# Mixture of experts in two parts: each token's row in DRAM goes from 130 to 144 values

## The chip, the cores and the metric

The kernel runs on one core of one Trainium2 chip. The metric is device time in microseconds (us) of one execution. The engines are named as in the profile: PE (matrix multiplication; PEld is its loading of weights), DVE (vector), ACT (activations), POOL (GpSimd), SP (which here only issues DMA transfers).

## The reference, cut to what matters

The program is four layers, each as `x = x + layernorm(layer(layernorm(x)))`, over 16 x 256 = 4096 tokens of 128 fp32 values: differential attention, two rounds of window attention with a feed-forward block, a state-space scan, and a mixture of experts. Only the last one is touched:

```python
xt = x.reshape(-1, D)                        # 4096 tokens, D = 128
logits = xt @ router_w.T                     # 8 experts
topk_vals, topk_idx = jax.lax.top_k(logits, TOP_K)          # TOP_K = 2
g = jax.nn.sigmoid(topk_vals)
g = g / (g.sum(axis=-1, keepdims=True) + 1e-10)
for e in range(E):                                          # E = 8, H = 256
    ge = jnp.sum(jnp.where(topk_idx == e, g, jnp.zeros_like(g)), axis=-1)
    h = jax.nn.silu(xt @ w_gate[e]) * (xt @ w_up[e])
    out = out + ge[:, None] * (h @ w_down[e])
```

## The kernel before

A token goes to two of eight experts, so the kernel sorts tokens by expert through DRAM. It holds 32 tiles of 128 tokens, in eight groups of four tiles; groups 0 to 4 are part 0, groups 5 to 7 part 1.

**The row.** What is sorted is a row of `ROW = D + 2 = 130` fp32 values, 520 bytes: the 128 normalised values of the token (written by ACT into the tile `pay`, L647 called from `outer_apply`), the token's number (column 128, written for all tokens by one DVE copy, L1881) and the number of its first expert (column 129, written by DVE in `choose`, L1753). The DRAM tensor `mx_rows` has 9 x 4096 = 36864 such rows: a region for each expert in each part, and one spare for slots that hold no expert's tile.

**The fill.** Before the sorting, all rows of `mx_rows` are set to a blank row: SP issues nine transfers (L2301) of 4096 rows each from the tile `mx_blank` during the first layer, right behind the loads of the weights. POOL waits for all nine (`filled`) before it sends the first token row.

**Sending.** In the mixture DVE, PE and ACT work out group by group where each token's two rows go (`choose`, `place`, `ranks`). POOL then issues eight indirect transfers a group (L1662), each of which writes 128 rows from `pay` to the rows that `mx_posu` names: 64 such transfers in all. Between groups POOL raises variances to the power -1/2 for two layernorms (L620), which ACT needs for the next groups' rows.

**The experts.** A table that DVE makes lists 80 slots: for each, an expert and the 128 rows that it works on. SP loads slot i (L1613: 128 rows into one of 16 buffers of the ring `mx_xin`) once the part's rows have been sent (`sent`), and from the 17th on once the buffer's former tile has been turned by PE (`x_full`) and its numbers read by DVE (`aimed`, L1848 to L1853). PE turns two tiles at a time (L2095), ACT moves them out of PSUM (L1965), then come gate and up (PE L2102, ACT L1973, DVE L1860), the turning of h (PE L2110, ACT L1979), down (PE L2120), and DVE's move of the result into `mx_y` (L1867). POOL writes the result by an indirect transfer of 128 rows of 512 bytes into `mx_results` (L1692). Sends of the last group and a half stand between POOL's first slots.

**The end.** When all results of a part have landed, SP fetches them (L1619, L1620), ACT and DVE weigh, sum and normalise them, and SP stores the output (L1624).

All orders are written out by hand, one program for each engine; each waits on semaphores only. There is no scheduler.

Of the kernel before, what the change touches and what calls it, by code (L numbers as in the profile page):

```python
# [12 lines left out]
D = 128  # L13
# [78 lines left out]
def apart(eng, scratch):  # L92

    eng.tensor_tensor(scratch, scratch, scratch, ALU.mult)
# [1366 lines left out]

ROW = D + 2
PAD = 1e6
FIRST = (0, 5, GROUPS)
PART_TILES = [NT * (FIRST[p + 1] - FIRST[p]) for p in range(2)]
# [22 lines left out]
def dispatch_constants(sb):  # L1491
    c = {}
    for k, shape in (("tri", [P, P]), ("ones", [P, P]), ("region", [P, 2, NE]), ("upto", [P, NE, NE]),
                     ("tile_no", [P, SLOTS]), ("tile_rows", [P, TILES]), ("trash", [P, SLOTS]), ("blank", [P, ROW]),
                     ("token", [P, TILES])):
        c[k] = sb("mx_" + k, shape)
    for k, n in (("count", SLOTS), ("place", SLOTS), ("number", TILES)):
        c[k] = sb("mx_" + k, [P, n], I32)
    return c

def mixture_of_experts(nc, X, F, out, rows, results, consts, c, w, ws, states, filled, fills):
# [10 lines left out]
    with ExitStack() as ctx:  # L1513
# [6 lines left out]

        pay = sb("pay", [P, TILES, ROW])
        top = sb("top", [P, TILES, 8])
# [5 lines left out]
        idf = sb("idf", [P, TILES, 2])  # L1528
# [21 lines left out]
        targetu = sb("targetu", [P, SLOTS], U32)  # L1550
        xin = sb("xin", [P, RING, ROW])
        xT = sb("xT", [P, 2, 2, P])
# [14 lines left out]
        applied, added, paid, first_named = (sem(n) for n in ("applied", "added", "paid", "first_named"))  # L1567
# [17 lines left out]
        def of(g):  # L1585
            return slice(g * NT, (g + 1) * NT)

        def part_of(g):
            return 0 if g < FIRST[1] else 1

        def seen_at(g):

            return g + part_of(g)
# [17 lines left out]
        def _(sp):  # L1611
# [16 lines left out]
            for part in range(2):  # L1628
                sp.wait_ge(listed, part + 1)
                for i in range(START[part], START[part + 1]):  # L1630
                    if i % SHARE == 0:
                        _, values = nc.values_load_multi_w_load_instructions(
                            c["place"][0:1, i:i + SHARE], engines=(mybir.EngineType.SP,), min_val=0,
                            max_val=(NE + 1) * TILES * P - P, skip_runtime_bounds_check_because=BOUND)
                        for k, v in enumerate(values):
                            at[i + k] = v
                    if i == START[part]:
                        sp.wait_ge(sent[part], 16 * 2 * PART_TILES[part])
                    if i >= RING:
                        sp.wait_ge(x_full, (i - RING) // 2 + 1)  # L1640
                        sp.wait_ge(aimed, (i - RING) // SHARE + 1)
                    load(i)
                    if i == START[1] + RING + 2:
                        fetch(0)
# [66 lines left out]
        def _(dve):  # L1711
            own_steps = Steps(dve, own)

            def outputs(g):

                for b in (2 * g, 2 * g + 1):
                    dve.wait_ge(o_full, b + 1)
                    dve.tensor_tensor(F[:, QT + b * QT:QT + (b + 1) * QT, :],
                                      psO[:, b % 2, 0:T].rearrange("p (t n) -> p t n", t=QT),
                                      dv[:, :].unsqueeze(1).broadcast_to([P, QT, D]), ALU.add).then_inc(o_used, 1)  # L1720
                dve.wait_ge(o_used, 2 * g + 2)
                inner.statistics(dve, g)
# [8 lines left out]
            def choose(g):  # L1731

                dve.wait_ge(r_full, g + 1)
                ins = dve.tensor_copy(lo[:, of(g), :], psR[:, 0:NT * NE].rearrange("p (t e) -> p t e", t=NT))
                ins.then_inc(r_used, 1)
                dve.wait_ge(r_used, g + 1)
                apart(dve, APART["dve"])
                for t in range(g * NT, (g + 1) * NT):
                    ins = dve.max(top[:, t, :], lo[:, t, :])
                own_steps.mark(ins)  # L1740
                own_steps.last()
                apart(dve, APART["dve"])
                for t in range(g * NT, (g + 1) * NT):
                    ins = dve.max_index(idx[:, t, :], top[:, t, :], lo[:, t, :])
                own_steps.mark(ins)
                own_steps.last()
                own_steps.mark(dve.tensor_copy(idf[:, of(g), :], idx[:, of(g), 0:2]))
                own_steps.last()
                own_steps.mark(dve.tensor_tensor(
                    hot[:, g, :, :, :], eid[:, :].unsqueeze(1).unsqueeze(1).broadcast_to([P, 2, NT, NE]),  # L1750
                    idf[:, of(g), :].rearrange("p t c -> p c t").unsqueeze(3).broadcast_to([P, 2, NT, NE]),
                    ALU.is_equal))
                dve.tensor_copy(pay[:, of(g), D + 1:ROW], idf[:, of(g), 0:1]).then_inc(first_named, 1)  # L1753
                own_steps.last()
                dve.tensor_tensor(both[:, g, :, :], hot[:, g, 0, :, :], hot[:, g, 1, :, :], ALU.add)\
                   .then_inc(hot_ready, 1)
                dve.wait_ge(hot_ready, g + 1)
                own_steps.mark(dve.tensor_reduce(inc[:, g, :], both[:, g, :, :].rearrange("p t e -> p e t"),
                                                 axis=AX.X, op=ALU.add))
                own_steps.last()  # L1760
                dve.tensor_tensor(seen[:, seen_at(g) + 1, :], seen[:, seen_at(g), :], inc[:, g, :], ALU.add)\
                   .then_inc(seen_ready, 1)
# [115 lines left out]

            dve.memset(seen[:, 0, :], 0.0)
            dve.memset(seen[:, seen_at(FIRST[1]), :], 0.0).then_inc(seen_ready, 1)  # L1880
            dve.tensor_copy(pay[:, :, D:D + 1], c["token"][:, :].unsqueeze(2)).then_inc(numbered, 1)  # L1881
            outputs(0)
            outputs(1)
# [8 lines left out]
            outer.shifts(dve, 1)  # L1892
            residual(2)
            choose(0)
            place(0)
            for g in range(FIRST[1]):
                outer.shifts(dve, g + 2)
                inner.shifts(dve, g + 3)
                choose(g + 1)
                if g + 4 < GROUPS:  # L1900
                    outputs(g + 4)
                place(g + 1)
                if g + 2 == FIRST[1]:
                    need_tiles(0)
                    tiles_of_experts(0)
                    rows_of_tiles(0)
                residual(g + 3)
            gates(0)
            choose(LATE - 1)
            place(LATE - 1)  # L1910
            outer.shifts(dve, LATE)

            gate_up(0)
            for i in range(SLOTS + 1):
# [18 lines left out]
                if i - 5 in SUM_AT:  # L1933
                    g = SUM_AT[i - 5]
# [97 lines left out]
        def _(pe):  # L2032
# [46 lines left out]
            def load_experts(n):  # L2079
                _, values = nc.values_load_multi_w_load_instructions(  # L2080
                    c["count"][0:1, n * SHARE:(n + 1) * SHARE], engines=(mybir.EngineType.PE,), min_val=0,
                    max_val=NE - 1, skip_runtime_bounds_check_because=BOUND)
                for k, v in enumerate(values):
                    chosen[n * SHARE + k] = v
# [79 lines left out]
def build(nc, ins, consts_in, out, stop=None):  # L2164
    with ExitStack() as ctx:
# [64 lines left out]
        mx = dispatch_constants(sb)  # L2230
        rows = nc.dram_tensor("mx_rows", ((NE + 1) * TILES * P, ROW), FP32).ap()
        results = nc.dram_tensor("mx_results", (2 * TILES * P + SLOTS * P, D), FP32).ap()
# [3 lines left out]
        with nc.Block() as block:  # L2236
# [7 lines left out]
            def _(pool):  # L2244
# [8 lines left out]
                pool.memset(mx["blank"][:, D:D + 1], PAD)  # L2253
                pool.memset(mx["blank"][:, D + 1:ROW], -1.0).then_inc(blanked, 1)
                pool.memset(mx["ones"][:, :], 1.0)
# [174 lines left out]
```

## Time and profile before

| | |
|---|---|
| Time before, median of 3 runs | 2056.2 us (2054.87 to 2056.44) |
| The profiled execution's own time | 2068.7 us |
| Its span, first to last instruction | 2066.9 us |
| PE, DVE, ACT, POOL busy | 84%, 75%, 66%, 43% of the span |
| The mixture of experts in the span | from about 1765 us to the end |
| TensorE clock granted, mean | 0.925 |

The profile is of one execution, which took 12.5 us longer than the median of the timed runs. The shares of busy time are means over four layers with different limits; for this change what counts is the fill, which lies in the first layer, and the last 300 us.

### The profile page before, as it was taken

How to read it: one execution, taken by the hardware profiler on the slowest of the kernel's cores; microseconds unless marked ns; L12 is line 12 of the kernel's file. 1: busy time of each engine (PE TensorE's matmuls, PEld its weight loads, DVE VectorE, ACT ScalarE, POOL GpSimd, SP SyncE). 2: the span in 40 equal slices, each digit the busy share in tenths (PEclk: the TensorE clock that was granted, in tenths of full speed). 3: DMA queues.
4: the chain of work that ended last, by engine and by line, in shares of the span. 5: the costliest groups of instructions: out<-in, count | busy, mean ns of one | idle time of the engine just before them, and what ended most of it. 6: DMA issues, size and time to landing. Idle time of an engine off the chain costs nothing. (4 is left out here: it accounts for less than half of the span.)

```text
span 2066.9 us, 39567 instructions
## 1 busy us (share of the span) xinstructions
PE 1733.7 (84%) x12418; PEld 1135.9 (55%) x12484; DVE 1555.1 (75%) x4202; ACT 1371.4 (66%) x4730; POOL 880.0 (43%) x819
## 2 busy tenths in 40 slices
PE   4999999999999945999998786999997765647883
PEld 2555555555555523777776443777776432544552
DVE  2988889988889866999996565999996564753353
ACT  2888888888888853888886224888886235323454
POOL 3555655556555543333332123333332122475553
PEclk9999999999999977999999897999999897659996
DMA  7990000000000000000000100000000100012242
GB/s 206 189 183 2 2 2 2 2 2 2 1 2 2 2 0 6 16 12 16 16 11 20 30 14 6 16 11 17 17 13 19 30 13 1 16 54 78 76 115 77
DMA packets 103935, 66.98 MB, mean 32 GB/s; under 512 B 27954, under 2 KB 95154, under 8 KB 103730
## 3 DMA queue, kind: packets, MB, share of 16 engines
q1 hardware_dynamic: 99122, 54.94, 13.2%
q0 software_dynamic: 4608, 9.51, 1.4%
q8 instruction: 104, 1.70, 0.4%
q14 instruction: 101, 0.83, 0.1%
HBM read 20.03 MB, written 30.77 MB: 25 GB/s over the span
## 5 line engine op out<-in xcount | busy, mean ns | idle before, releaser
L411 ACT ACTIVATE a_E<-a_psS,a_nm 128x128 f32<-128x128 f32 (+1 forms) x1028 | 419.8, 429 | 31.0 <-DVE a_nm L245 28.4
L216 POOL TENSOR_SCALAR a_aT<-a_dT 128x384 f32<-128x384 f32 x256 | 310.1, 1211 | 298.8 <-PE a_psO L529 187.3
L245 DVE TENSOR_REDUCE a_nm<-a_psS 128x2 f32<-128x256 f32 (+1 forms) x514 | 260.2, 547 | 44.7 <-PE a_psS L496 44.1
L492 PE MATMUL a_psS<-a_kT,a_qm 32*128 32x128 f32 (+1 forms) x2064 | 240.6, 351 | 5.7 <-issue 3.7
L270 DVE SCALAR_TENSOR_TENSOR a_d<-a_E,a_cf 128x128 f32<-128x128 f32 (+1 forms) x512 | 218.7, 468 | 28.1 <-DVE a_cf L259 1.9
L411 ACT ACTIVATION_READ_ACCUMULATOR a_E<-a_psS,a_nm 128x1 f32 x1028 | 220.3, 214 | 0.0
L830 POOL TENSOR_TENSOR b1rn<-b1ss,minus_half 128x16 f32<-128x16 f32 x36 | 107.2, 2977 | 223.5 <-DVE b1ss L866 223.5
L830 POOL TENSOR_TENSOR b0rn<-b0ss,minus_half 128x16 f32<-128x16 f32 x36 | 107.2, 2977 | 221.9 <-DVE b0ss L866 221.9
L420 ACT ACTIVATE a_dT<-a_psT 128x384 f32<-128x384 f32 x256 | 127.0, 496 | 74.6 <-PE a_psT L505 72.0
L492 PEld LDWEIGHTS a_psS<-a_kT,a_qm 32*128 32x128 f32 x2064 | 136.6, 186 | 56.1 <-issue 36.0
L505 PE MATMUL a_psT<-ident,a_d 128*128 128x128 f32 x768 | 132.2, 281 | 6.6 <-DVE a_d L270 0.5
L1692 POOL DMA_INDIRECT mx_results<-mx_y,mx_targetu x80 | 77.2, 965 | 74.1 <-DVE mx_y L1867 57.2
L505 PEld LDWEIGHTS a_psT<-ident,a_d 128*128 128x128 f32 x768 | 87.7, 141 | 35.0 <-DVE a_d L270 29.0
L496 PE MATMUL a_psS<-causal,identb 128*128 128x256 bf16 x516 | 101.9, 279 | 0.0
L964 ACT ACTIVATE b0E<-b0psS,b0nm 128x128 f32<-128x128 f32 x260 | 92.0, 377 | 10.0 <-DVE b0nm L894 10.0
L964 ACT ACTIVATE b1E<-b1psS,b1nm 128x128 f32<-128x128 f32 x260 | 92.0, 377 | 8.7 <-DVE b1nm L894 8.7
L1077 PE MATMUL b0psQ<-wqk,b0hT 128*128 128x512 f32 x148 | 80.5, 670 | 17.0 <-DVE b0part L875 12.0
L1077 PE MATMUL b1psQ<-wqk,b1hT 128*128 128x512 f32 x148 | 80.6, 670 | 16.8 <-DVE b1part L875 11.3
L2102 PE MATMUL mx_psG<-m_experts,mx_xT 128*128 x160 | 85.8, 619 | 8.8 <-ACT mx_xT L1965 8.5
L1860 DVE TENSOR_TENSOR mx_h<-mx_psG,mx_sl 128x256 f32<-128x256 f32 x80 | 33.9, 424 | 75.6 <-ACT mx_sl L1973 43.3
L1046 PEld LDWEIGHTS b1psS<-b1kT,b1qm 128*128 128x128 f32 x528 | 71.8, 197 | 18.2 <-issue 16.3
L518 PE MATMUL a_psO<-a_dT,a_vp 128*32 128x256 f32 x516 | 81.2, 393 | 0.6 <-ACT a_dT L420 0.6
(359 smaller groups left out, 4425.4 us busy)
## 6 DMA issues: line engine op xcount, KB each, us to landing
mx_rows<-mx_blank SPq DMA_DIRECT2D x9, 2080.0 KB, 30.8
mx_xin<-mx_rows SPq DMA_DIRECT2D x80, 65.0 KB
b0v<-b0v SPq DMA_DIRECT2D x34, 128.0 KB, 2.3
b1v<-b1v SPq DMA_DIRECT2D x34, 128.0 KB
F<-mx_results SPq DMA_DIRECT2D x8, 256.0 KB, 4.6
mx_second<-mx_results SPq DMA_DIRECT2D x8, 256.0 KB, 5.0
out_dram<-X SPq DMA_DIRECT2D x8, 256.0 KB, 2.4
mx_results<-mx_y,mx_targetu POOLq DMA_INDIRECT x80
```

The costliest lines, as they stand in the source:

```text
L216: pool.tensor_scalar(aT[:, s, :], dT[:, s, :], 0.0, None, ALU.max).then_inc(positived.sem, 1)
L245: ins = dve.tensor_reduce(nm[:, s, t, :], psS[:, s, :, (0, P)[t]:(P, 384)[t]], axis=AX.X, op=ALU.max, negate=True)
L270: ins = dve.scalar_tensor_tensor(out=d[:, s, c0:c1], in0=E[:, s, 1, c0:c1], scalar=cf[:, s, t:t + 1], in1=E[:, s, 0, c0:c1], op0=ALU.mult, ...
L411: ins = act.activation(E[:, s, m, c0:c1], psS[:, s, m, c0:c1], ACT.Exp, bias=nm[:, s, t, m:m + 1], accum_out=Z[:, p, h, t, m:m + 1])
L420: act.activation(dT[:, s, :], psT[:, s, 0:384], ACT.Copy).then_inc(evaced.sem, 1)
L492: pe.matmul(psS[:, s, m, c0:c1], qm[rows, p, a, r, t * P:(t + 1) * P], kT[rows, p, a, 0:c1 - c0], start=(t == 0), stop=False)
L496: ins = pe.matmul(diagonal, identb[:, :], causal[:, :].unsqueeze(1).broadcast_to([P, 2, P]), start=False, stop=True)
L505: ins = pe.transpose(psT[:, s, c * P:(c + 1) * P], d[:, s, c * P:(c + 1) * P], ident[:, :])
L830: pool.tensor_tensor(rn[:, t, :], ss[:, t, :], minus_half[:, 0:2 * H], ALU.pow).then_inc(rn_ready.sem, 1)
L964: ins = act.activation(E[:, s, n, :], psS[:, s, n * P:(n + 1) * P], ACT.Exp, bias=nm[:, s, n:n + 1], accum_out=Z[:, s, n:n + 1])
L1077: ins = pe.matmul(psQ[:, n * W:(n + 1) * W], hT[:, p, t * P:(t + 1) * P], wqk[:, n * W:(n + 1) * W], start=True, stop=True)
L2102: pe.matmul(psG[:, i % 2, :], xT[:, i // 2 % 2, i % 2, :], of_expert(i, 0, DOWN), start=True, stop=True)\
```

## The change

`ROW` becomes `D + 16 = 144` values, 576 bytes, in `mx_rows`, `pay`, `mx_blank` and `mx_xin`. Columns 130 to 143 carry nothing. Column 129 is now addressed as one column instead of as the rest of the row, and a new DVE memset at the start of the mixture sets the 14 new columns of all 32 tiles of `pay` to zero. The memset of `mx_blank`'s last columns (POOL, at the start of the program) becomes 15 columns wide instead of one.

```diff
-ROW = D + 2
+ROW = D + 16
...
-                dve.tensor_copy(pay[:, of(g), D + 1:ROW], idf[:, of(g), 0:1]).then_inc(first_named, 1)
+                dve.tensor_copy(pay[:, of(g), D + 1:D + 2], idf[:, of(g), 0:1]).then_inc(first_named, 1)
...
             dve.memset(seen[:, 0, :], 0.0)
             dve.memset(seen[:, seen_at(FIRST[1]), :], 0.0).then_inc(seen_ready, 1)
+            dve.memset(pay[:, :, D + 2:ROW], 0.0)
             dve.tensor_copy(pay[:, :, D:D + 1], c["token"][:, :].unsqueeze(2)).then_inc(numbered, 1)
```

The order of instructions is the same on every engine but for this one on DVE. The piece of the difference below is DVE's at the start of the mixture; 128x32x14 is partitions, tiles and new columns.

```order
 L1879 MEMSET mx_seen 128x8
 L1880 MEMSET mx_seen 128x8
-L1881 COPY mx_pay<-mx_token 128x32
+L1881 MEMSET mx_pay 128x32x14
+L1882 COPY mx_pay<-mx_token 128x32
 L1718 TENSOR_TENSOR F<-mx_psY,s_wD 128x256 x2
```

The memset has come between the two small ones and the copy of the tokens' numbers; everything behind it moves down one line. The transfers are as many as before, in the same places: 9 of the fill, 64 sends, 80 loads, all with 144 values a row in place of 130.

## Rows read from the trace of the kernel before

**Rows 1.** The page: span, busy time and share of the engines, DMA queues.

```profile
span 2066.9 us, 39567 instructions
PE 1733.7 (84%) x12418; PEld 1135.9 (55%) x12484; DVE 1555.1 (75%) x4202; ACT 1371.4 (66%) x4730; POOL 880.0 (43%) x819
...
q1 hardware_dynamic: 99122, 54.94, 13.2%
q0 software_dynamic: 4608, 9.51, 1.4%
```

**Rows 2.** The chain that ended last: start, length, what.

```profile
1789.56 1.24 POOL mx_rows L1662
...
1835.78 0.97 POOL mx_rows L1662
...
2036.15 0.96 POOL mx_results L1692
```

**Rows 3.** Timeline from part 0's last send to PE's first expert tile.

```profile
1849.40 0.96 POOL L1662 DMA_INDIRECT mx_rows<-mx_pay,mx_posu  x1 [0.30 <-issue]
...
1851.85 20.07 SPq L1613 DMA_DIRECT2D mx_xin<-mx_rows  x16
...
1858.41 1.11 PE L2048 MATMUL mx_psX<-ident,mx_pay 128*128 128x128 f32 x4 [2.75 <-issue]
...
1863.94 2.07 PE L2102 MATMUL mx_psG<-m_experts,mx_xT 128*128 x2 [3.98 <-ACT mx_xT L1965]
```

**Rows 4.** Timeline of PE where the loop over slots has no pauses.

```profile
1973.20 0.38 PE L2095 MATMUL mx_psT<-ident,mx_xin 128*128 128x128 f32 x2
...
1979.75 0.38 PE L2095 MATMUL mx_psT<-ident,mx_xin 128*128 128x128 f32 x2
```

**Rows 5.** ACT's waits, 1866 to 2034 us: total us, times, longest.

```profile
ACT mx_xT L1965 <- PE mx_psT L2095: 11.2, 20, 1.6
...
ACT mx_xT L1965 <- remote: 5.2, 3, 2.3
```

**Rows 6.** SP's waits, 1780 us to the end: total us, times, longest.

```profile
SPq L1641 <- DVE mx_targetu L1853: 21.5, 4, 8.7
```

**Rows 7.** Timeline of SP, the fill's issues.

```profile
46.60 95.05 SPq L2301 DMA_DIRECT2D mx_rows<-mx_blank  x9
```

**Rows 8.** DMA queue, 90 to 150 us: packets, MB, share of 16 engines.

```profile
q1 hardware_dynamic: 21482, 11.13, 123.0%
```

**Rows 9.** L411, ACT's exponentials: stretch, us, busy (count), PEclk, DMA share, GB/s.

```profile
83.40:126.90 43.50, 27.59 (x128) 1.00 1.26 186
213.90:257.40 43.50, 27.63 (x129) 1.00 0.01 2
```

**Rows 10.** Timeline of DVE at the mixture's start.

```profile
1765.70 0.07 DVE L1879 MEMSET mx_seen<- 128x8 f32 x1 [0.64 <-PEq L1362]
1765.72 0.20 DVE L1881 COPY mx_pay<-mx_token 128x32 f32<-128x32 f32 x1
...
1766.38 0.87 DVE L1718 TENSOR_TENSOR F<-mx_psY,s_wD 128x256 f32<-128x256 f32 x2 [0.46 <-PE mx_psY L2039]
```

**Rows 11.** Groups by form: busy us, mean ns, idle before.

```profile
L918 DVE MEMSET b0qm<- 128x4096 f32 x1 | 3.5, 3472 | 0.8 <-issue 0.8
...
L336 DVE MEMSET a_psO<- 128x256 f32 x1 | 0.3, 272 | 0.4 <-PEq L2236 0.4
...
L1692 POOL DMA_INDIRECT mx_results<-mx_y,mx_targetu x80 | 77.2, 965 | 74.1 <-DVE mx_y L1867 57.2 <-issue 16.9
```

**Rows 12.** The sends' line: ns least/median/most, first and last start.

```profile
L1662 POOL DMA_INDIRECT mx_rows<-mx_pay,mx_posu x64: 957/962/1299, 1789.6 to 1946.0; - x64
```

**Rows 13.** DMA queue, 1852 to 1878 us, loads of `mx_xin`: columns as above.

```profile
q1 hardware_dynamic: 3024, 1.40, 25.5%
```

**Rows 14.** DMA queue, 2058 to 2062 us, stores of 512-byte rows.

```profile
q1 hardware_dynamic: 773, 0.38, 33.6%
```

**Rows 15.** DMA queue, 1851.8 to 1855 us.

```profile
q1 hardware_dynamic: 554, 0.26, 45.5%
```

## The prediction

> **What bounds the kernel now.** I start with the page. PE is busy for 84% of the span and the rows' transfers for little: the queue that carries the fill and the loads took 13.2% of the time of 16 DMA engines, the queue of POOL's indirect transfers 1.4% [rows 1]. These are means over four layers, and only two stretches hold the changed rows: the fill in the first layer, and the mixture from 1765 us on. So the chain of work that ended last comes next. In the mixture it first runs through POOL: from 1789.56 us to the end of the piece at 1835.78 it is POOL issuing sends and, between groups, raising variances to a power. It then passes to DVE, PE and ACT, and in the experts mostly through PE, until POOL's last result at 2036.15 us [rows 2].
>
> The reader should look at two places. The first is the hand-over from sending to experts. Part 0's last send is issued by 1850.36 us (1849.40 + 0.96), SP issues the first load at 1851.85, PE still turns the last group of tokens at 1858.41, and its first expert matmul starts at 1863.94 [rows 3]. The second is the loop over slots. Where it has no pauses PE turns a pair of tiles, and four tiles later another: 1979.75 - 1973.20 = 6.55 us, 1.64 us a tile [rows 4]. For 80 tiles that is 131 us, but the loop goes from 1863.94 to 2037.11 us, 173 us. The 42 us between are pauses and added work. A part that could have to do with loaded rows is ACT's wait for the turned tiles, 11.2 us in 20 waits and another 5.2 us whose releaser the trace does not tell [rows 5]. SP itself is ahead of PE there: its waits before a load are 21.5 us on DVE's numbers of a share eight tiles back [rows 6], so a load is issued many tiles before its use.
>
> **The fill.** Nine transfers with 36864 rows in all are issued by SP from 46.60 us for 95 us [rows 7]. From 90 to 150 us there is little else: 123.0% of 16 engines x 60 us over 21482 packets is 55.0 ns a packet, one row each, and 36864 of them take 103 us [rows 8]. The trace has no row of 576 bytes. Lower bound: the stores of 512-byte rows took 33.6% x 16 x 4 us / 773 = 27.8 ns a packet [rows 14]; scaled to 576 bytes 31.3 ns, a fill of 59 us. Upper bound: 55.0 x 576/520 = 60.9 ns, 114 us. I take no value between, because neither costs anything: POOL waits for the fill only before its first send at 1789.56 us, and the attention beside the fill keeps its pace. In a stretch of 43.5 us ACT did 128 exponentials in 27.59 us with the DMA share at 1.26, and 129 in 27.63 us with it at 0.01 [rows 9]. If that cover were gone the fill would cost its own change, -44 to +11 us; nothing in the rows makes it go.
>
> **The memset.** It writes 32 x 14 = 448 values a partition on DVE. Two memsets give the slope: 272 ns for 256 values, 3472 ns for 4096, 0.833 ns a value, so 448 values take 0.43 us [rows 11]. Upper bound: short runs may cost more; the copy behind it, with 32 runs of one value, takes 0.20 us, and adding that whole gives 0.63 us. DVE now idles 0.46 us, waiting for PE, between that copy and its first real work at 1766.38 [rows 10]. So 0 to 0.17 us shows; I take 0.05 us and count it in full. Behind it stands DVE's first sum and with it all of the mixture, so a memset that outlasts the cover delays everything by what is over. POOL's memset of 15 columns in place of one lies at the program's start, beside the loads of the inputs: nothing.
>
> **The sends.** Of 64, 32 lie on the chain (four groups of eight between 1789.56 and 1836 us) [rows 2]. Each holds POOL for 962 ns at 520 bytes a row [rows 12]; the indirect transfers of 512-byte rows take 965 ns in the mean [rows 11]. POOL's time goes by rows and not by bytes as far as these two sizes tell, and both have 128 rows. I take nothing. Upper bound: a time in proportion to bytes would be 962 x 56/520 = 0.10 us a send, 3.3 us for 32 and 4.1 us for part 0's 40. A gain is excluded on POOL: shorter rows were no cheaper.
>
> **The loads and landings.** A load gives each of 16 engines eight rows. From 1852 to 1878 us a packet took 25.5% x 16 x 26 us / 3024 = 35.1 ns [rows 13], a load 0.28 us of an engine. With the bounds of above it becomes 8 x 31.3 = 0.25 us or 8 x 38.9 (35.1 x 576/520) = 0.31 us: -0.03 to +0.03 us. I take 0 for the loads, since they are ahead of PE. The first ones are the closest: by 1855 us 554 packets, some four loads of 128 rows, had moved [rows 15], and PE is not free before 1858.41 [rows 3], so 3 us cover a change of hundredths. The last send's landing is as short a piece, eight rows an engine at 6 ns more, 0.05 us, behind the same cover; I add it as the only other term.
>
> The Trainium skill speaks against the pad here ("DMA: Bandwidth & Descriptors", section "How a descriptor splits into AXI transactions"): a read is charged in beats of 32 bytes from the 256-byte boundary below its start. By my estimate from that page, rows of 520 bytes, whose starts move by 8 bytes, cost 20.5 beats in the mean, and rows of 576 bytes, whose starts move by 64, cost 21.0; alignment to 64 bytes would then buy nothing on reads, and a load would go from 0.28 to 0.29 us. The stores above, aligned to 512 bytes, are cheaper per packet than either kind of 520-byte row, which fits an alignment cost but does not say that 64 bytes are enough. By page or by row the sum is the same to 0.1 us.
>
> **Sum.** 0.05 + 0.05 = 0.1 us. The profiled execution took 2068.7 us and would take 2068.8. It is 12.5 us above the median of the runs, of which I know no cause in these terms, so I carry the difference over unscaled: 2056.2 + 0.1 = 2056.3 us. A measurement of this kernel tells about 0.2%, 4 us, from no change.
>
> **Rivals.**
>
> *Everything hidden (the forecast), 0.80.* It includes the case that the padding does not do what it is for, that packets take as long a byte as before, since neither end of the packets' price reaches the end of the program. Its own range is -1 to +1.5 us: 2055 to 2058.
>
> *Slower: POOL's sends grow with the row, 0.08.* The place is L1662 on the chain. It decides from 4.1 us / 32 = 0.13 us a send. Against it stand the two equal durations; for it, that 512 and 520 bytes are so near that they exclude no step above them. In proportion to bytes it gives 2059.6 to 2060.4 us, just short of telling; if a row of 576 bytes were written as two pieces and a send cost twice 0.96 us, 32 x 0.96 = 31 us and 2087 us.
>
> *Faster: late rows are behind part of the loop's pauses, 0.12.* The waits for turned tiles are 16.4 us [rows 5], the loop's loss 42 us. Rows of 55 and 35 ns beside 28 ns say that something about 520-byte rows is dear, and if their transfers also held up completions that PE waits for, a quarter to a half of 16.4 us would go: 2048 to 2052 us. Against it: SP is 8 tiles or more ahead [rows 6], that is 8 x 1.64 = 13 us for a transfer of 0.3 us, and the loop runs without pauses at 1973 us.
>
> **How the numbers follow.** The likeliest case gives 2056.3 us. From the range I leave out the double send and the farther half of the faster case, together about 1 in 8: 2050.5 to 2061 us. Faster by over 0.2% is 0.10: of the third case 0.02 stay within, at its 2052 us. Slower is 0.06: of the second case 0.02 stay within, at 2059.6 us. Within is the rest, 0.84.
>
> **What would show it.** In the profile of the changed kernel: a DVE memset of about 0.43 us at the mixture's start, with the first sum (L1718) at most 0.2 us later behind it; sends still at 0.96 us; a fill of 36864 rows at 31 to 61 ns each, with the attention's stretches unchanged; first load about 1.5 us behind the last send; the pause-free loop still at 1.64 us a tile. The prediction is wrong if sends are longer than 1.06 us, if the waits of ACT for turned tiles fall or rise by more than 4 us, or if the attention beside the fill moves by more than 1 us in 43.5.

## The result: 0.36% faster, through a layer that the diff does not name

| | before | after |
|---|---|---|
| Median | 2055.7 us (6 runs, 2054.87 to 2056.57) | 2047.84 us (6 runs, 2046.78 to 2050.49) |
| Ratio, 95% interval | | 0.9964 [0.9951, 0.9977] |
| Profiled execution | 2068.7 us | 2049.57 us |

The forecast was no change. The time fell by 7.9 us, past the low end of the range by 2.7 us.

First the page of the changed kernel, beside [rows 1].

```profile
span 2047.8 us, 39568 instructions
PE 1736.7 (85%) x12418; PEld 1142.2 (56%) x12484; DVE 1553.2 (76%) x4203; ACT 1371.8 (67%) x4730; POOL 879.9 (43%) x819
...
q1 hardware_dynamic: 99122, 57.58, 10.9%
q0 software_dynamic: 4608, 9.97, 1.5%
```

More bytes took less of the DMA engines' time: 10.9% in place of 13.2%. The padding does make the fill cheaper. The next three views are SP's timeline at the fill, the queue from 60 to 100 us, and ACT's exponentials beside and behind the fill, the first and third as in [rows 7] and [rows 9].

```profile
47.26 68.21 SPq L2302 DMA_DIRECT2D mx_rows<-mx_blank  x9
```
```profile
q1 hardware_dynamic: 20554, 11.79, 113.8%
```
```profile
83.40:126.90 43.50, 27.63 (x129) 1.00 1.04 273
213.90:257.40 43.50, 27.60 (x128) 1.00 0.01 2
```

The issues of the fill take 27 us less, and a packet takes 113.8% x 16 x 40 / 20554 = 35.4 ns. But the attention beside the fill has the pace that it has without one, so none of this reaches the end.

DVE at the mixture's start, the sends' line, and the hand-over to the loads, beside [rows 10, 12, 3]:

```profile
1763.78 0.07 DVE L1879 MEMSET mx_seen<- 128x8 f32 x1 [0.64 <-PEq L1362]
...
1763.93 0.43 DVE L1881 MEMSET mx_pay<- 128x448 f32 x1
1764.28 0.13 DVE L1882 COPY mx_pay<-mx_token 128x32 f32<-128x32 f32 x1
1764.46 0.87 DVE L1718 TENSOR_TENSOR F<-mx_psY,s_wD 128x256 f32<-128x256 f32 x2
```
```profile
L1662 POOL DMA_INDIRECT mx_rows<-mx_pay,mx_posu x64: 957/962/1301, 1787.6 to 1927.5; - x64
```
```profile
1847.47 0.96 POOL L1662 DMA_INDIRECT mx_rows<-mx_pay,mx_posu  x1 [0.30 <-issue]
```
```profile
1849.96 1.96 SPq L1613 DMA_DIRECT2D mx_xin<-mx_rows  x4
```

From the first memset to the first sum it is 0.68 us, as before. A send is 962 ns, as before. From part 0's last send to the first load it is 2.49 us against 2.45. The stages that the prediction looked at are as it said. So where did 7.9 us come from?

**A trap in the pair of profiles.** The two spans differ by 19.1 us, and the loop over slots seems to give most of it. These are the rows of that loop, from the first to the last gate matmul: before, after, and then two kernels from the experiments, one that gains (z alone moved) and one that doesn't (mixture alone moved).

```profile
1863.94:2031.88 167.94, 141.66 (x722) 89.56 (x723) 76.99 (x298) 81.93 (x237) 92.12 (x96) 0.98 0.31 87
```
```profile
1857.40:2012.62 155.22, 143.22 (x721) 94.43 (x722) 75.10 (x298) 82.28 (x237) 95.85 (x99) 0.93 0.35 99
```
```profile
1856.37:2030.50 174.13, 148.21 (x721) 94.81 (x722) 76.40 (x298) 82.64 (x237) 94.21 (x98) 0.93 0.30 85
```
```profile
1864.34:2019.81 155.47, 143.52 (x722) 94.48 (x723) 74.95 (x298) 82.45 (x237) 95.63 (x99) 0.93 0.33 95
```

Over all profiles the loop, from the start of the first gate matmul to the start of the last, is 155 us or 168 to 178 us long. Among the sixteen profiles of the experiments, which of the two it is went with the set of kernels that shared a chip, not with the kernel. In the two sets in which the kernel before had medians of 2076.2 and 2074.3 us, all eight profiles show the long loop; in the two with 2052.9 and 2054.0 us, all eight show the short one. The 12.7 us between the first pair look like such a difference and no part of the 7.9 us: the kernel before, whose profile has the long loop, took 2055.7 us as the median of its runs, like the sets with the short one. What makes the loop long in a set is not known. What the timed runs tell from one another had to be found with kernels timed side by side.

### The profile page after: what moved, and what is told of

It is laid out like the page before. It is cut to its first block and busy times, and to the rows that moved or that the text cites. A ratio compares the mean times of both kernels' runs of the same rounds, so it can differ in the third digit from the quotient of the medians.

```text
span 2047.8 us, 39568 instructions
## 1 busy us (share of the span) xinstructions
PE 1736.7 (85%) x12418; PEld 1142.2 (56%) x12484; DVE 1553.2 (76%) x4203; ACT 1371.8 (67%) x4730; POOL 879.9 (43%) x819
## 3 DMA queue, kind: packets, MB, share of 16 engines
q1 hardware_dynamic: 99122, 57.58, 10.9%
## 5 line engine op out<-in xcount | busy, mean ns | idle before, releaser
L411 ACT ACTIVATE a_E<-a_psS,a_nm 128x128 f32<-128x128 f32 (+1 forms) x1028 | 419.9, 429 | 30.4 <-DVE a_nm L245 27.8
L411 ACT ACTIVATION_READ_ACCUMULATOR a_E<-a_psS,a_nm 128x1 f32 x1028 | 220.5, 215 | 0.0
L1046 PEld LDWEIGHTS b0psS<-b0kT,b0qm 128*128 128x128 f32 x528 | 71.9, 197 | 18.2 <-issue 16.3
```

Of the source, the lines that this page charges most:

```text
L411: ins = act.activation(E[:, s, m, c0:c1], psS[:, s, m, c0:c1], ACT.Exp, bias=nm[:, s, t, m:m + 1], accum_out=Z[:, p, h, t, m:m + 1])
```

## The experiments

Ratios are to runs of the kernel before on the same chip.

### Padded rows in DRAM, or padded tiles in SBUF?

The kernel before once more, for the resolution of what follows.

> The kernel before, unchanged, as the measure of what a repeat does. All theories: ratio 1.000 within 0.001. Its profile also tells whether the pauses of the loop over slots (41 us above 1.64 us a tile in the first profile, with SP instructions of 0.7 us) belong to the kernel or to that one profiled execution: if to the kernel, the loop again takes about 168 us from first to last gate matmul; if to the execution, some 10 us less.

Measured: 0.9996 [0.9986, 1.0006]. Its loop over slots took 170.2 us, so by the expectation the pauses would belong to the kernel. The sets with the short loop show that one repeat was not enough to say so: there a kernel whose mixture has other places in SBUF and nothing else changed took 155.5 us.

Wide tiles, narrow rows in DRAM:

```diff
+WIDE = D + 16
-... ("blank", [P, ROW]),
+... ("blank", [P, WIDE]),
-        pay = sb("pay", [P, TILES, ROW])
+        pay = sb("pay", [P, TILES, WIDE])
-        xin = sb("xin", [P, RING, ROW])
+        xin = sb("xin", [P, RING, WIDE])
```

with the memsets of the change, and every transfer moving columns 0 to 129 alone.

> The rows in DRAM keep 130 values and every transfer moves 130; only the tiles in SBUF are 144 wide, with the new memset, so all tiles lie where the change puts them. Theory A (the gain comes from rows that start and end on 64 bytes in DRAM): ratio 1.000, fill at 55 ns a row. Theory B (the gain comes from where the tiles lie in SBUF, 32 bytes and more further on): ratio 0.996, fill at 55 ns a row.

Measured: 0.9967 [0.9954, 0.9980]. The whole gain is there with 520-byte rows in DRAM.

Rows of 568 bytes (`ROW = D + 14`):

> The change with 14 new values a row (142, 568 bytes: 8 bytes short of a multiple of 64) in place of 16. Theory A (64-byte multiples in DRAM): ratio 1.000 or a little above, a fill of 55 ns a row or more, 60 ns at most. Theory B (place in SBUF): 0.996. A third theory, that wider rows help by themselves: 0.996 with the fill's price anything.

Measured: 0.9970 [0.9957, 0.9982].

Rows of 544 bytes (`ROW = D + 8`):

> The change with 8 new columns... 136 values a row, 544 bytes, a multiple of 32 bytes but not of 64. Theory A in its 64-byte form: like 130 values, ratio 1.000, fill about 55 ns a row. If 32 bytes are enough: ratio 0.996 and a fill of about 31 ns a row, as with 144. Theory B (place in SBUF): 0.996 whatever the fill.

Measured: 1.0004 [0.9993, 1.0015]. No account by the alignment of DRAM rows sorts these: 520 in DRAM gains, 568 gains, 544 does not, although its fill is cheap too (37.6 ns a row). Theory B as written missed the last one as well: it took for granted that 136 values also move the tiles. With 576 every tile of the layers, all allocated behind it, stands 32 bytes further: what started 32 bytes past a multiple of 64 now starts at one, and the other way round.

### Is it the place of the later tiles?

An unused tile of 32 bytes does the move by itself. In the kernel before:

```diff
         mx = dispatch_constants(sb)
+        sb("gap32", [P, 8])
```

> The kernel before (rows of 130 values, no memset) with one unused tile of 32 bytes a partition right behind the dispatch constants, so that every tile after it lies 32 bytes further in SBUF, as in the changed kernel. Theory P (the place of the later tiles in SBUF is what counts): ratio 0.9965 to 0.997, below 0.998. Theory D (the padded rows and their transfers count): 1.000 within 0.001. Theory L (what counts is the larger tile itself, or its memset): 1.000.

Measured: 0.9954 [0.9941, 0.9967]. The same line in the changed kernel, which takes the move back:

> The changed kernel (rows of 144 values, memset) with the same 32-byte tile, so that every later tile is back at the place modulo 64 bytes that it had before the change. Theory P: the gain is gone, ratio 1.000 within 0.001. Theory D and theory L: the gain stays, 0.9965.

Measured: 0.9998 [0.9989, 1.0006]. Its fill is the cheap one (36864 rows in about the same 68 us) and its memset is there. This is the change as the prediction saw it, and it is worth nothing. Theory P holds; theories D and L fall. (Theories have new letters in each group of experiments; each expectation says what its letters mean.)

### Which layer, which tile?

The gap at the start of the mixture's stack only:

> The kernel before with a 32-byte tile at the start of the mixture's stack alone: only the mixture's tiles move by 32 bytes. If the mixture's tiles carry the gain of theory P: 0.997. If the layers ahead do: 1.000; if the mixture loses by the move and the others gain, over 1.000. Theory D: 1.000.

Measured: 0.9999 [0.9989, 1.0009]. The gap around the other layers:

```diff
-        differential_attention(nc, X, consts, wA, load_later)
+        with nc.sbuf_tensor("gap32a", [P, 8], FP32):
+            differential_attention(nc, X, consts, wA, load_later)
...
+            with nc.sbuf_tensor("gap32b", [P, 8], FP32):
                 normalise_all(nc, "n0", X, F, minus_half)
                 for l in range(2):
                     window_attention(nc, f"b{l}", F, consts, wB[l])
...
                     feed_forward(nc, f"f{l}", F, consts, wF[l])
```

> The kernel before with a 32-byte tile around the attention and around the window and feed-forward layers alone: their tiles move by 32 bytes, those of the state-space layer and of the mixture stay. If these layers carry the gain of theory P: 0.997, with the feed-forward layers near 95.9 us instead of 98.2 and a window layer near 362.1 us instead of 363.6 in the profile. If the mixture does: 1.000. Theory D: 1.000.

Measured: 0.9966 [0.9953, 0.9979]. The gain lies ahead of the mixture. In the profiles the feed-forward layers differ, and the first difference in them is their start. There SP brings the first tokens from the tile `F` into the tile `z` in three transfers: half of the channels straight, the other half one token further, and the token that this leaves over. DVE can't begin before they land. SP's, DVE's and PE's timelines at the start of the first feed-forward layer in the kernel before:

```profile
1131.47 0.71 SPq L1222 DMA_DIRECT2D f0z<-F  x1
1132.23 0.87 SPq L1223 DMA_DIRECT2D f0z<-F  x1
1133.15 7.00 SPq L1224 DMA_DIRECT2D f0z<-F  x1
```
```profile
1143.03 0.87 DVE L1257 BATCH_NORM_STATS2 f0st<-f0z 128x6 f32<-128x128 f32 x4 [12.61 <-DMA f0z<-F]
```
```profile
1146.89 1.11 PE L1322 MATMUL f0psX<-ident,f0xn 128*128 128x128 f32 x4 [16.93 <-DVE f0xn L1272]
```

And in the changed kernel:

```profile
1135.19 0.71 SPq L1222 DMA_DIRECT2D f0z<-F  x1
1135.95 0.87 SPq L1223 DMA_DIRECT2D f0z<-F  x1
1136.87 6.50 SPq L1224 DMA_DIRECT2D f0z<-F  x1
```
```profile
1145.46 0.87 DVE L1257 BATCH_NORM_STATS2 f0st<-f0z 128x6 f32<-128x128 f32 x4 [11.32 <-DMA f0z<-F]
```
```profile
1149.32 1.11 PE L1322 MATMUL f0psX<-ident,f0xn 128*128 128x128 f32 x4 [15.65 <-DVE f0xn L1272]
```

From the first issue to DVE's statistics: 11.56 us before, 10.27 after. The rest of the way to PE is the same 3.86 us. `z` is the first tile of its layer; by the sizes of the tiles ahead of it, it starts 32 bytes past a multiple of 64 in the kernel before and at a multiple in the changed one. So `z` alone was moved, with the tiles behind it put back:

```diff
+        sb("gapa", [P, 8])
         z = sb("z", [P, 2, NT, D])
+        sb("gapb", [P, 8])
         st = sb("st", [P, NT, 6])
```

> The kernel before with 32 bytes ahead of the tile z of each feed-forward layer and 32 bytes behind it: z, the target of that layer's transfers from F, starts at a multiple of 64 bytes, and every other tile keeps its place modulo 64. Theory Z (rows of 256 bytes that DMA writes to a place 32 bytes off a multiple of 64 cost more, and each feed-forward layer starts with them): z's first landing 1.3 us earlier, with the slower clock behind it some 2.2 us less per layer, ratio 0.9978 to 0.998, all that the feed-forward layers have to give. Theory A (engines read or write their tiles at another pace at the other place): 1.000, since no other tile moves.

Measured: 0.9968 [0.9958, 0.9978]. Everything moved except `z`:

> The kernel before with every tile after the dispatch constants moved by 32 bytes except the tile z of the feed-forward layers, which stays at 32 modulo 64. Theory Z: 4.4 us short of the kernel with all tiles moved, ratio 0.9975 to 0.998, with the feed-forward layers at 98.2 us as before. Theory A: 0.9955, as with all tiles moved.

Measured: 0.9989 [0.9978, 1.0000]. The window layers alone:

> The kernel before with the tiles of the two window layers alone moved by 32 bytes, the V tile that their 128 KB copies write among them. The rest of the gain of 7 to 9 us, if it lies in these layers: ratio 0.9985 (3 us). If the copies' landings are hidden and the window layers differ only by where the slower clock falls: 1.000 within 0.0008.

Measured: 1.0009 [0.9999, 1.0018]. The feed-forward layers alone:

> The kernel before with all tiles of the two feed-forward layers moved by 32 bytes, and no others (z at a multiple of 64, the tiles behind it at 32). Theory Z: the same as with z alone, 0.9978 to 0.998. Theory A: lower than with z alone, by what the tiles of hidden values give.

Measured: 0.9973 [0.9961, 0.9986]. One tile carries most of the gain: theory Z holds, and theory A (the engines' pace at the tiles), which asked for 1.000 with `z` alone moved and 0.9955 with `z` held, falls. The sizes were missed. `z` alone gave more than the 0.9978 to 0.998 expected, and holding `z` left less of a gain than the 0.9975 to 0.998 expected: the landing comes 1.3 us sooner, as expected, but the layers gain more than the 2.2 us each that were counted (their lengths stand further down). Read in the same way in every profile, the way from the first issue to the statistics in the first feed-forward layer is 11.55 to 11.59 us in the seven kernels with `z` at 32 modulo 64, and 10.26 to 10.29 us in the seven with `z` at 0 and the transfer whole. There is nothing between. In the second layer it is 11.38 to 11.40 and 10.10 to 10.11 us.

### Why so much, and there only?

For most of that way the DMA engines do almost nothing. The next two rows (stretch, us, five engines idle, granted clock, DMA share, GB/s) are of 3 us while the one-token-further transfer runs: the kernel before, then the one with `z` alone moved.

```profile
1137.00:1140.00 3.00, 0.00 (x0) 0.00 (x0) 0.00 (x0) 0.00 (x0) 0.00 (x0) 0.50 0.08 16
```
```profile
1138.00:1141.00 3.00, 0.00 (x0) 0.00 (x0) 0.00 (x0) 0.00 (x0) 0.00 (x0) 0.50 0.08 18
```

A share of 0.08 is little more than one engine of 16 (0.0625). The transfer goes from 127 partitions to 127, in 508 rows of 256 bytes, one behind another. They are not dearer from the start. Next are the queue's packets in 1 us early in the transfer (1135.6 to 1136.6 us before, 1136.83 to 1137.83 with `z` alone moved), then in 3.5 us late in it (1137.5 to 1141 and 1138.5 to 1142), each time the kernel before first.

```profile
q1 hardware_dynamic: 71, 0.02, 8.0%
```
```profile
q1 hardware_dynamic: 71, 0.02, 8.0%
```
```profile
q1 hardware_dynamic: 215, 0.05, 7.9%
```
```profile
q1 hardware_dynamic: 250, 0.06, 8.0%
```

Early on a row takes 14.1 ns in both. Later it takes 16.3 ns before and 14.0 ns with `z` moved. In the trace of the kernel before the pace changes behind about the 220th row, at 1137.1 us; for the 290 rows left the difference is 290 x 2.3 = 0.67 us. (One packet in four takes 28 ns there and the others 18 or 19, where with `z` moved all take 18.) The other 0.6 us lies behind the last row. The packets of 4 bytes that close the transfers start 10.40 us after the first issue before and 9.74 us with `z` moved; the semaphore's last increment follows 1.13 and 0.52 us later, at 11.53 and 10.26 us. Why the pace changes in mid-transfer, and why the increment comes later, no row tells. `F`, the source, has one place in all runs, so they also do not tell whether the place of `z` counts by itself or against that of `F`.

Why is it one engine? The Trainium skill says how this comes about ("DMA: Bandwidth & Descriptors", section "Why a DMA increments its semaphore by 16 and not by 1"): a transfer issued from SP uses the largest number of engines up to 16 that divides its outermost dimension, which for 127 partitions is one. The trace agrees with one: the share is 0.08, and where the first transfer (128 partitions) closes with 16 packets of 4 bytes, this one and the left-over token's together close with three. Giving it as two transfers tests that (the wait now counts four transfers in place of three):

```diff
-                sp.dma_start(z[1:P, p, :, 64:D], fs[0:P - 1, :, 64:D]).then_inc(done, 16)
+                sp.dma_start(z[1:113, p, :, 64:D], fs[0:113 - 1, :, 64:D]).then_inc(done, 16)
+                sp.dma_start(z[113:P, p, :, 64:D], fs[113 - 1:P - 1, :, 64:D]).then_inc(done, 16)
...
-            eng.wait_ge(shifted[half % 2], (pair + half // 2) * 48 + 48)
+            eng.wait_ge(shifted[half % 2], (pair + half // 2) * 64 + 64)
```

> The kernel before, z in its old place, with the feed-forward layers' transfer into partitions 1 to 127 given as two, 1 to 112 (448 rows, a multiple of 16) and 113 to 127 (60 rows). Theory O: 448 rows spread over 16 engines and 60 on one, 0.9 us in place of 508 at some 15.7 ns; from the first issue to the first statistics some 5 us in place of 11.56, the DMA share near 0.07 for 1 us and not for 9, ratio 0.993 to 0.995. Theory Q (the rows were spread already, the third transfer's issue is the wait): still 11 us or more, since there is one transfer more, ratio 1.000 or above.

Measured: 0.9912 [0.9896, 0.9928]. SP's and DVE's timelines in the first feed-forward layer:

```profile
1136.15 0.71 SPq L1222 DMA_DIRECT2D f0z<-F  x1
1136.91 0.73 SPq L1223 DMA_DIRECT2D f0z<-F  x1
1137.69 1.06 SPq L1224 DMA_DIRECT2D f0z<-F  x1
1138.80 0.71 SPq L1225 DMA_DIRECT2D f0z<-F  x1
```
```profile
1140.49 0.87 DVE L1258 BATCH_NORM_STATS2 f0st<-f0z 128x6 f32<-128x128 f32 x4 [5.39 <-DMA f0z<-F]
```

The statistics come 4.34 us after the first issue, 7.2 us sooner, and the 7 us for which SP held the transfer behind are gone. The gain is larger than expected (0.993 to 0.995): two landings 7.2 us sooner are 14.4 us, and the kernel gained 18. From first issue to last instruction the two feed-forward layers take 91.20 and 89.75 us in place of 98.35 and 98.36, 15.8 us less together. The same split with `z` at a multiple of 64:

> The same split with z at a multiple of 64 bytes. Theory O: the place is now worth 60 rows at 1.5 to 2.5 ns, 0.1 to 0.15 us a layer in place of 1.28, so within 0.1% of e_split: 0.993 to 0.995. If the place is worth as much as before whatever the split: 0.003 below e_split.

Measured: 0.9909 [0.9896, 0.9923], the way 4.34 us. Once the rows are spread, the place of `z` makes no difference that can be measured. Split at 65 (64 and 63 partitions):

> The kernel before with that transfer given as partitions 1 to 64 (256 rows, spread) and 65 to 127 (252 rows, not a multiple of 16). Theory O: 252 rows on one engine, some 4 us: the first statistics some 8 us after the first issue, halfway between the kernel before and e_split, ratio 0.996 to 0.9975. Theory Q: as for e_split, 1.000 or above.

Measured: 0.9907 [0.9891, 0.9923], the way 4.25 us. Theory O as I wrote it fails here: it asked for a number of rows that is a multiple of 16 and put 252 rows on one engine. By that rule of the Trainium skill 63 partitions use nine engines, 112 use 16, 15 use 15 and 127 one. The traces agree. These are the queue's packets in the 3.3 us from 1.3 us after the first issue on, split at 113 (1137.45 to 1140.75) and at 65 (1136.99 to 1140.29):

```profile
q1 hardware_dynamic: 1071, 0.26, 39.4%
```
```profile
q1 hardware_dynamic: 1065, 0.26, 40.4%
```

Of these 512 + 508 + 2 = 1022 are rows. The other 49 and 43 are packets of 4 bytes, in order of time 16, 16, 15 and 2 for the four transfers, and 16, 16, 9 and 2. Theory Q falls with all of these.

The whole move together with the split at 113:

> Rows of 130 values, every tile moved by 32 bytes as in the changed kernel, and the split at 112. Theory O: 0.993 to 0.995, faster than the changed kernel by 5 us or more. Theory Q: 0.9955 or above.

Measured: 0.9914 [0.9898, 0.9929]: 2034.83 us beside 2053.95 of the kernel before. Each of the four versions with the split beats the kernel before by some 0.9%, without padding. Against the changed kernel, at 0.9964 of the kernel before, that would be some 0.5%; it was not timed beside them.

## Why the prediction was wrong

**What failed** is the step from which the sum was made: the list of what the change does. It had the fill, the memset, the sends, the loads and the landings. Of `mx_blank` it said only that its memset lies at the program's start, "nothing". It did not ask what else a wider tile moves. `mx_blank` is allocated ahead of the tiles of all layers, grew from 544 to 576 bytes, and with that moved the target of the transfers with which each feed-forward layer starts, and for which all engines wait, by 32 bytes. The missing term is 11.56 - 10.27 = 1.3 us at the start of each feed-forward layer, and what the clock makes of it. PE's windows show that, from its first matmul to the rise of the clock and behind it, before and then after:

```profile
1146.89:1154.16 7.27, 6.40 (x11) 2.84 (x12) 1.49 (x10) 3.44 (x4) 0.57 (x1) 0.50 0.15 32
1154.16:1160.00 5.84, 5.19 (x28) 3.19 (x27) 3.60 (x7) 1.46 (x2) 1.71 (x2) 1.00 0.12 25
```
```profile
1149.32:1155.10 5.78, 4.91 (x9) 2.44 (x10) 1.43 (x10) 2.75 (x3) 0.00 (x0) 0.50 0.17 37
1155.10:1160.00 4.90, 4.24 (x14) 1.80 (x14) 3.59 (x8) 2.15 (x3) 2.25 (x2) 1.00 0.08 18
```

PE had idled while `z` landed, and its granted clock was at the lower level (1.2 GHz). After the first matmul it stays there for 7.27 us before and 5.78 us after. From the first issue to the layer's last instruction the first feed-forward layer takes 98.35 us before and 96.15 after, 2.2 us less; the second 98.36 and 95.80. In three of the other profiles with `z` at 32 (the kernel before again, rows of 544, window layers moved) the second one takes 99.8 to 99.9 us: there the granted clock rises sooner but falls to 0.5 once more (1623.51 to 1626.92 us in the kernel before again). So a layer gives 2.2 to 4.1 us, both together 4.8 to 6.5 us, where `z` alone measured (1 - 0.9968) x 2074.3 = 6.6 us [4.6 to 8.7]. What remains up to the 7.9 us of the change is within the intervals; a further tile with a small share can't be excluded, as `z` held back still left 0.9989 [0.9978, 1.0000].

**What was right,** each term with what it measured:

- The fill hidden, 31 to 61 ns a row: 35.4 ns, and ACT's busy time beside it 27.63 us against 27.60.
- The memset 0.43 us, with 0 to 0.17 us showing and 0.05 counted: 0.43 us, and nothing showing (0.68 us from the first memset to the first sum, before and after).
- The sends unchanged: 962 ns. The rival of longer sends is refuted at 576 bytes.
- Loads 0 and the last landing 0.05 us: the first load starts 2.49 us after the last send in place of 2.45, 0.04 us.
- All of it together: the changed kernel with the tiles put back measured 0.9998 [0.9989, 1.0006] where the sum said 1.00005.

**The rival "faster"** (0.12; 2048 to 2052 us) had the sign and nearly the time, by luck: its mechanism is not what happened. Neither late rows nor the loop's pauses are in it. Its sign to watch, the waits of ACT for turned tiles, was a poor one: they are 10.8 us after against 11.2 us before [rows 5], and the 5.2 us beside them are gone after, but also in the kernel that gained nothing (tiles put back). That is the difference between sets of runs again.

## What to carry to other kernels

- Before summing what an edit costs, list what it moves. A tile's size sets the addresses of all tiles allocated behind it; to test an idea about a size, put a filler tile in to hold the other addresses still. Here the idea measured 0.9998 and its side effect, the move without the padding, 0.9954.
- Look in the DMA share for a stretch in which everything waits and the share stands at one engine of 16: there a transfer runs on one engine, and a partition count such as 127 given as two transfers brought the first statistics 7.2 us forward in each of two layers, and the kernel gained 0.9%.
- Do not read the difference of two kernels from one profile of each: here 12.7 us of 19.1 us came and went with the set of runs, while the place of `z` gave 1.3 us at the start of each of two layers, the same in every profile.

## What the runs showed of the hardware

- Where one DMA engine wrote 508 rows of 256 bytes to SBUF, the first 220 or so took the same at both places (14.1 ns a row from 1135.6 to 1136.6 us). The later ones took 14.0 ns to places at multiples of 64 bytes and 16.3 ns to places 32 bytes off, and the semaphore's last increment came 0.52 and 1.13 us behind the closing packets. With the rows spread over more engines the place made no difference (4.34 us both times), nor did it for the 128 KB copies of the window layers' V (median landing 2.3 us in the kernel before and in the one with the window layers moved).
- Behind a transfer of 508 rows on one engine SP held its next one for 7.0 us, 6.5 us with `z` at a multiple of 64, and 1.06 us with the rows spread.
- The fill's rows in DRAM, from 60 to 100 us, for rows of 520 (the kernel before), 544 and 568 bytes:

```profile
q1 hardware_dynamic: 14236, 7.37, 124.9%
```
```profile
q1 hardware_dynamic: 20567, 11.15, 120.8%
```
```profile
q1 hardware_dynamic: 14800, 8.37, 114.6%
```

With 640 us of engine time (16 x 40) these are 56.2, 37.6 and 49.6 ns a row, beside 35.4 ns for 576 bytes. The 56.2 ns are high for 520 bytes: the eleven other kernels with such rows show 49.9 to 52.4 ns. Of these four sizes the two that are multiples of 32 bytes are cheap and the two that are multiples of 8 alone are dear; a multiple of 64, which 576 is and 544 is not, was not needed for it.
